# A transformer block on one core: moved DMA loads, a moved projection tile and a new order of carry, squares and SiLU

## The reference

```
x = x + layernorm(attn(layernorm(x)))      # no scale or shift in any layernorm
x = x + layernorm(ffn(layernorm(x)))

attn: q, k, v = split(x @ w_qkv.T + b_qkv) # 16 heads of 32
      per chunk of 128 tokens, state S (32 x 32 per head):
      inter = (q * decay_q) @ S
      intra = ((q @ k.T) * dmask) @ v
      S     = lam_c * S + (k * decay_k).T @ v
      out   = (inter + intra) @ w_out.T + b_out
ffn:  silu((x @ gate) * gs) * ((x @ up) * us) @ down * ds    # weights rounded to fp8 e4m3, inner width 1536
```

## Time and profile before

| | |
|---|---|
| median of 3 timed runs | 1053.86 us (1053.73 to 1054.44) |
| the profiled execution | 1055.15 us |
| its span, first to last instruction | 1053.4 us |
| PE busy with matmuls | 962.4 us, 91% |
| DVE, ACT, POOL busy | 684.1, 527.3, 687.5 us |
| mean granted TensorE clock | 0.98 of full speed |
| one slot in the steady state | 44.60 us |

### The profile page before, as it was taken

How to read it: one execution, slowest core, us unless ns; L and a number is a source line. 1 busy time by engine, 2 the same in 40 slices (tenths; PEclk the granted TensorE clock), 3 DMA queues, 4 the chain that set the end, 5 groups by cost and what they waited for, 6 DMA issues and landing times.

```text
span 1053.4 us, 21805 instructions
## 1 busy us (share of the span) xinstructions
PE 962.4 (91%) x8388; PEld 704.9 (67%) x8388; DVE 684.1 (65%) x1340; ACT 527.3 (50%) x997; POOL 687.5 (65%) x839
## 2 busy tenths in 40 slices
PE   1987989999777899999999999999999999999996
PEld 1755757777555577676776767767677686766764
DVE  6757766775475776576767657677766776756322
ACT  3534746675444554563545645456454464544421
POOL 2649887887555566685666857658576685856633
PEclk9988999999889899999999999999999999999999
DMA  9567889989999869387492864929559395621100
GB/s 341 134 206 202 247 210 227 245 209 216 244 226 229 162 136 191 76 156 128 107 189 76 165 118 114 184 75 170 112 123 166 87 169 112 130 61 41 38 24 21
DMA packets 297496, 159.79 MB, mean 152 GB/s; under 512 B 141616, under 2 KB 272688, under 8 KB 297264
## 3 DMA queue, kind: packets, MB, share of 16 engines
q1 hardware_dynamic: 296672, 157.86, 67.6%
q10 hardware_dynamic: 720, 0.54, 0.2%
HBM read 82.86 MB, written 41.94 MB: 118 GB/s over the span
## 4 chain that ended last, share of the span: by engine, by line
PE 58%; ACT 12%; DVE 9%; issue 8%; POOL 6%; SPq 5%; DMA 2%; POOLq 0%; DVEq 0%; ACTq 0%
PE bank L799 20%; PE bank L813 16%; PE att L776 8%; PE bank L707 4%; PE bank L692 4%; ACT w_pool L543 3%; PE att L692 3%; ACT y L441 2%; DVE w_pool L1329 2%; ACT hl L441 2%; ACT att_pool L497 2%; DVE stats L1198 2%; SPq L340 1%; DMA dram_qk<-qk_hl 1%; DVE state_hl L1269 1%
## 5 line engine op out<-in xcount | busy, mean ns | idle before, releaser
L799 PE MATMUL bank<-f_pool,gate_q 128*128 128x256 f16 x1536 | 184.2, 273 | 17.7 <-ACT w_pool L543 16.7
L799 PE MATMUL bank<-f_pool,up_q 128*128 128x256 f16 x1536 | 184.5, 274 | 0.0
L813 PE MATMUL bank<-down_q,w_pool 128*128 128x512 f16 x768 | 168.5, 379 | 11.0 <-DVE w_pool L1329 10.6
L799 PEld LDWEIGHTS bank<-f_pool,gate_q 128*128 128x128 f16 x1536 | 146.9, 98 | 41.8 <-ACT w_pool L543 21.0
L949 POOL TENSOR_TENSOR att_pool<-p,att_pool 128x512 f16<-128x512 f32 x128 | 145.7, 1161 | 39.1 <-ACT att_pool L497 39.1
L799 PEld LDWEIGHTS bank<-f_pool,up_q 128*128 128x128 f16 x1536 | 150.9, 98 | 18.0
L1329 DVE SCALAR_TENSOR_TENSOR w_pool<-bank,us_t,w_pool 128x256 f32<-128x256 f32 x192 | 84.1, 479 | 120.5 <-PE bank L799 70.6
L963 POOL TENSOR_TENSOR w_pool<-w_pool 128x512 f16<-128x512 f32 x96 | 111.8, 1164 | 65.8 <-ACT w_pool L549 65.8
L887 POOL TENSOR_TENSOR rstd<-mv,eps_t 128x1 f32<-128x1 f32 (+1 forms) x112 | 27.8, 248 | 176.8 <-DVE mv L1201 158.7
L813 PEld LDWEIGHTS bank<-down_q,w_pool 128*128 128x128 f16 x768 | 73.8, 98 | 99.9 <-DVE w_pool L1329 13.0
L497 ACT CAST att_pool<-p 128x512 f16<-128x512 f32 x128 | 75.6, 618 | 91.7 <-DVE p L1239 91.7
(11 more groups left out here) (139 smaller groups left out, 1823.1 us busy)
## 6 DMA issues: line engine op xcount, KB each, us to landing
xr<-in_x SPq DMA_DIRECT2D x32, 512.0 KB, 4.4
dram_qk<-qk_hl SPq DMA_DIRECT2D x64, 256.0 KB, 5.3
att_pool<-dram_qk SPq DMA_DIRECT2D x64, 256.0 KB, 6.8
f_pool<-dram_qk SPq DMA_DIRECT2D x64, 256.0 KB, 7.0
dram_v<-vv SPq DMA_DIRECT2D x32, 256.0 KB, 2.7
dram_kd<-kd_hl SPq DMA_DIRECT2D x32, 256.0 KB, 3.1
qn_pool<-dram_qk SPq DMA_DIRECT2D x32, 256.0 KB, 7.7
out_x<-w_pool SPq DMA_DIRECT2D x32, 256.0 KB, 2.1
```

The lines of the kernel that those rows point to most:

```text
L799: ins = nc.tensor.matmul(b[:, j * TOK:(j + 1) * TOK], w[:, k, o * P:(o + 1) * P], x1_hl[:, v % 2, part, k], start=(k == 0 and part == 0), ...
L813: ins = nc.tensor.matmul((b_gate, b_up)[t][:, :], h_hl[:, part, k, t * P:(t + 1) * P], down_q[:, k], start=(k == 0 and part == 0), stop=(k ...
```

## The change

No instruction of arithmetic is added or removed. Moved are:

- on SP, the load of unit 0 from behind lead block 12 to behind lead block 8, and the load of unit 1 from early call 0 to behind lead block 13;
- on PE, the sums of squares of pieces 0 to 4 by one block (5 joins 6 in block 8), and DVE's first maximum from block 6 to 7;
- in the early calls, ACT's k_hi ahead of y_normalise and x1_hi, POOL's residuals and x1_lo back, DVE's x1_moments behind carry and state;
- in a slot, the second tile of the output projection (`project(u, 1)`) behind `gate_up(v, 2)`, carry and state of the second chunk behind `gate_up(v, 4)`, SiLU ahead of y_normalise and x1_hi, state_hi and state_lo back; `down` waits for the last SiLU in place of the last product.

```diff
--- before.py
+++ after.py
@@ -204,6 +204,12 @@
         def squares(n):
             buf = o32 if n % 2 else y32
             return buf[:, :].rearrange("p t d -> p (t d)").bitcast(F16)[:, 0:I]
+
+
+
+        SUMMED = {3: (0,), 4: (1,), 5: (2,), 6: (3,), 7: (4,), 8: (5, 6), 9: (7,), 10: (8,), 11: (9,), 12: (10,),
+                  13: (11,)}
+        NORMS = {7: 0, 10: 1}
 
 
         def x_src(n):
@@ -397,8 +403,10 @@
             turn_x(1)
             for k in range(LEAD):
                 ahead(k)
-                if k == LEAD - 2:
+                if k == LEAD - 6:
                     load_unit(0)
+                if k == LEAD - 1:
+                    load_unit(1)
 
             for s in range(units + 2):
                 n, u, v = s + LEAD, s - 1, s - 2
@@ -408,7 +416,7 @@
                     spill_kd(n - 1)
                 if v >= 1:
                     store(v - 1, 0)
-                if s + 1 < units:
+                if 2 <= s + 1 < units:
                     load_unit(s + 1)
                 if v >= 1:
                     store(v - 1, 1)
@@ -595,17 +603,17 @@
                 q_hi(n, 0)
                 probs_hi(s, 0, 1)
                 q_hi(n, 1)
+                k_hi(n, 2)
                 if u >= 0:
                     y_normalise(u, 0)
                     y_normalise(u, 1)
-                k_hi(n, 2)
                 probs_hi(s, 1, 0)
+                k_hi(n, 3)
+                probs_hi(s, 1, 1)
+                state_hi(s, 1)
                 if u >= 0:
                     x1_hi(u, 0)
                     x1_hi(u, 1)
-                k_hi(n, 3)
-                probs_hi(s, 1, 1)
-                state_hi(s, 1)
                 o_hi(s)
 
             def slot(s):
@@ -626,27 +634,27 @@
                     probs_hi(s, 0, 1)
                 silu(v, 1)
                 h_hi(v, 1)
+                silu(v, 2)
                 if projects:
                     y_normalise(u, 0)
-                silu(v, 2)
+                h_hi(v, 2)
                 if projects:
                     y_normalise(u, 1)
-                h_hi(v, 2)
+                silu(v, 3)
                 if attends:
                     probs_hi(s, 1, 0)
-                silu(v, 3)
                 if projects:
                     x1_hi(u, 0)
                 h_hi(v, 3)
                 if attends:
                     probs_hi(s, 1, 1)
+                silu(v, 4)
                 if projects:
                     x1_hi(u, 1)
-                silu(v, 4)
-                if attends:
-                    state_hi(s, 1)
                 h_hi(v, 4)
                 silu(v, 5)
+                if attends:
+                    state_hi(s, 1)
                 h_hi(v, 5)
                 if attends:
                     o_hi(s)
@@ -803,7 +811,7 @@
 
             def down(v, t):
                 if t == 0:
-                    pe.wait_ge(h_d, 6 * v + 6)
+                    pe.wait_ge(silu_d, 6 * v + 6)
                     pe.wait_ge(h_lo_d, 6 * v + 5)
                 for k in range(IT):
                     if t == 0 and k == IT - 2:
@@ -820,8 +828,8 @@
                 project_qk(k, 1)
                 project_qk(k, 2)
                 project_qk(k, 3)
-                if 2 <= k < 14:
-                    sum_squares(k - 2)
+                for n in SUMMED.get(k, ()):
+                    sum_squares(n)
                 project_v(k, 0)
                 project_v(k, 1)
 
@@ -857,16 +865,18 @@
                 gate_up(v, 1)
                 if projects:
                     project(u, 0)
+                gate_up(v, 2)
+                if projects:
                     project(u, 1)
-                gate_up(v, 2)
                 if attends:
                     attend(s, 0)
                     scores(s, 1, 0)
                 gate_up(v, 3)
                 if attends:
                     scores(s, 1, 1)
+                gate_up(v, 4)
+                if attends:
                     carry_and_state(s, 1)
-                gate_up(v, 4)
                 gate_up(v, 5)
                 if attends:
                     attend(s, 1)
@@ -1016,18 +1026,17 @@
                 if u >= 0:
                     for t in range(T):
                         inverse_std_of(LN_Y, u, t)
-                    for t in range(T):
-                        residual(u, t)
+                state_decay(s, 1)
                 probs_lo(s, 1, 0)
                 if u >= 0:
                     for t in range(T):
-                        inverse_std_of(LN_X1, u, t)
-                state_decay(s, 1)
-                if u >= 0:
-                    x1_lo(u, 0)
+                        residual(u, t)
                 probs_lo(s, 1, 1)
                 if u >= 0:
-                    x1_lo(u, 1)
+                    for t in range(T):
+                        inverse_std_of(LN_X1, u, t)
+                    for t in range(T):
+                        x1_lo(u, t)
 
             def slot(s):
                 n, u, v = s + LEAD, s - 1, s - 2
@@ -1357,10 +1366,8 @@
                     scale_wout()
                 if k == 5:
                     split_wout()
-                if k == 6:
-                    norms(0)
-                if k == 10:
-                    norms(1)
+                if k in NORMS:
+                    norms(NORMS[k])
                 k_lo(k, 2)
                 if k < 12:
                     rounded(k)
@@ -1389,16 +1396,17 @@
                 k_lo(n, 2)
                 out_sum(s, 0)
                 masked(s, 1, 0)
-                if u >= 0:
-                    for t in range(T):
-                        x1_moments(u, t)
                 k_lo(n, 3)
                 masked(s, 1, 1)
                 v_sum(n, 0)
                 carry_and_state(s, 1)
+                if u >= 0:
+                    x1_moments(u, 0)
+                v_sum(n, 1)
+                if u >= 0:
+                    x1_moments(u, 1)
+                state_lo(s, 1)
                 o_max(s, 0)
-                v_sum(n, 1)
-                state_lo(s, 1)
                 out_sum(s, 1)
                 o_max(s, 1)
                 scale_o(s)
@@ -1421,8 +1429,9 @@
                 product(v, 1)
                 if projects:
                     y_moments(u, 0)
+                product(v, 2)
+                if projects:
                     y_moments(u, 1)
-                product(v, 2)
                 if projects:
                     x1_moments(u, 0)
                 if attends:
@@ -1433,16 +1442,16 @@
                 product(v, 3)
                 if attends:
                     masked(s, 1, 1)
-                    carry_and_state(s, 1)
                     o_max(s, 0)
                 product(v, 4)
                 if attends:
-                    state_lo(s, 1)
+                    carry_and_state(s, 1)
                 product(v, 5)
                 if attends:
                     out_sum(s, 1)
                     o_max(s, 1)
                     scale_o(s)
+                    state_lo(s, 1)
                     o_lo(s)
                 y2_scale(v, 0)
                 y2_moments(v, 0)
```

More of the change, by code:

```diff
@@ L642, in slot @@
                     probs_hi(s, 1, 1)
+                silu(v, 4)
                 if projects:
                     x1_hi(u, 1)
-                silu(v, 4)
+                h_hi(v, 4)
+                silu(v, 5)
                 if attends:
                     state_hi(s, 1)
-                h_hi(v, 4)
-                silu(v, 5)
                 h_hi(v, 5)
```

## The result

The changed kernel takes **1089.5 us** (median of 4 runs, 1089.13 to 1090.43) against 1053.8 us: ratio 1.034, 95% interval 1.032 to 1.036. The span went from 1053.4 to 1087.7 us, +34.3. The direction and the range held (1062 to 1094); the middle, 1080, was 9.5 us low, and the result lies 1.5 us outside the range of the likeliest case alone.

The account below looks back on a forecast made before the run. TensorE bounds the slots, with GpSimd's list nearly dense up to `down`. Loads +14, early calls -17.6, slots +29.3, slot 16 +1.7 and slot 17 -1.1 sum to +26 on 1053.9: 1080 us, range 1062 to 1094.

Parts of the forecast that it names:

- likeliest case: Slots, loads and early calls as forecast: 1080 us, range 1070 to 1088 taken alone, chance 0.6.
- Slots (b): Second projection tile behind block 2 ends 3.50 us later, GpSimd's list follows, `down` starts later: +2.14 us a slot.
- Slots (a): `down` waits for the last SiLU, state_lo and carry moved: both TensorE slot waits go, at most 1.86 us a slot.
- Loads: Lead blocks: early load of unit 0 delays spills, TensorE waits 12 us at block 10's squares; +14, bounds 9 and 18.
- Squares (c): Lead blocks: squares summed a block later take 3 waits away (11.9 us), costed at nothing.
- Slot 16: Slot that only projects: same GpSimd chain without probabilities, about +1.7 us.
- Early calls and slot 2 (d): Early calls into slot 2: earlier loads and k_hi cut TensorE's idle time; -17.6 us, bounds -10 and -26.
- The port rule: VectorE with two SBUF inputs and GpSimd lock each other out; moving state_lo would give VectorE 2.15 us a slot.
- The hidden load: Rival: slots as forecast, but the load behind lead block 8 is hidden; 1066 us, chance 0.15.
- The faster case: Rival: GpSimd's chain doesn't hold `down`, only the wait at attend stays, -0.85 us a slot; 1035 us, chance 0.12.
- The extra 1 us a slot: Rival: VectorE, waiting for the residual, makes GpSimd wait, 1 us more a slot; 1094 us, chance 0.1.
- the clock drop in a slot: Rival: new waits of about 1 us lower the clock in the slots; little chance, no time of its own.

Follow-up runs that it names:

- the version without the losses: The change with projection joined, y_normalise as before, h_lo(4) ahead of x1_lo(1), unit 0 loaded in pieces behind spills: 1014.4 us, 0.962; also called the best version.
- the experiment: The change with the order of ScalarE, GpSimd and VectorE in the two early calls as before: 1092.3 us, 1.037.

## Why the prediction was right, and where it missed

**Slots (b), +2.14 a slot.** Right, by the mechanism named. Measured +29.7 against +29.3 over 13 slots; the period is 46.70 as forecast, with waits of 0.93 for y (0.85), 1.43 for p (1.4) and 0.96 for the low half (1.1), and none at block 5. The slots that end a sequence lost more than the others, as worked out: 2.70 us each (forecast 2.5), against 2.10 in the others (2.14). The experiment with h_lo ahead of x1_lo shows that POOL's list is what holds `down` in the change: it takes out 1.10 us a slot, and nothing else was touched.

**Slots (a), "by themselves remove both slot waits: at most 1.86 us a slot".** Wrong as a description of the edit, harmless in the sum. Mean slot from `down` of slot 2 to `down` of slot 15, over kernels whose slots differ in these two things (their lead blocks and early calls differ too, but lie ahead of this stretch):

| order of the rest | projection joined | projection split |
|---|---|---|
| as before | 44.21 | 47.70 |
| the change's | 44.63 | 46.50 |
| the change's, y_normalise as before | 43.08 | 46.52 |

The split costs 3.44 us in the bottom row, one block (3.50): there POOL's list comes last with and without it. It costs 1.87 in the middle row, where y_normalise had already delayed that list. The 3.49 of the old order go another way, over ACT and DVE, with POOL's list done 1.4 us ahead of `down`. The rest of the order is worth 1.1 us when y_normalise stays where it was, and costs 0.4 when it moves behind h_hi(2); with the split it gives 1.2 in either form. I had the sum right since I worked it from the end of the second tile down POOL's list, and with the split nothing in the new order delays that list. The part for (a) by itself was not 1.86 but a loss of 0.4. To gain the two waits of a full slot takes y_normalise in its old place (44.60 to 43.23) and h_lo(4) ahead of x1_lo(1) as well (42.71 in the version without the losses, 1.89 less).

**Loads.** Right: 15.9 against 14, one wait of 13.46 where I had 12, behind v_hi and dram_v as named. The spill went out at 215.52 (214.9), the squares ended at 229.81 + 1.48 = 231.3 (229.8), and these 1.5 us are the wait that I had too short. The slow V projection cost 1.5 us where I had 2.3, and the squares' own matmuls 0.6 (1.46 for 0.82) where I had nothing. That the load causes it is shown twice: alone it makes +15.5, and back in its place it gives back 8 us net, with the wait at the squares gone.

**Squares (c), nothing.** Right: 1089.5 with and without. With the load late again the lead blocks end at 271.88 - 1.50 = 270.38, 2.2 us ahead of the kernel before, so without the stall the squares may be worth something. As kernels with the same lead blocks end them up to 2.0 us apart, that is not shown.

**Slot 16, +1.7.** Near in size (+1.3), but not by the chain named; that is luck. `down` waits 0.18 us for POOL there. PE loses its time to blocks 4 and 5, whose SiLU stand behind y_normalise and x1_hi in ACT's list: 3.4 us of waits in all, where before it had 1.49 and 0.97.

**Early calls and slot 2 (d), -17.6.** The step that failed, in size: -11.3. To block 0 of slot 2 I laid out 64 us; it took 355.16 - 288.40 = 66.8. For slot 2 I had 4.8 less and 2.1 more; it is 38.01 against 37.13 us, 0.9 more. What I missed is one transfer with two that wait for it. I had the chain from the last state over x1_hi and x1_lo to the turn, but took block 0 as held by little; it was held 5.10 us, and the lower clock made the first 16 matmuls 1.7 us longer. And I didn't see that ACT's o_hi waits for that same turn, so that SiLU 0 and 1 were late as well: PE waits 0.92 us at block 1 and 0.52 us at block 2. These and the slow matmuls are 3.1 of the 3.6 us that I had too little in slot 2. Of the -11.3, the load of unit 0 alone is worth -6.9 (116.07 to 109.15). With the load of unit 1 early and the change's slot order besides, it is 107.10 (-2.1), and the new order of the early calls brings 104.77 (-2.3). So the early order pays, and my reading in the experiment that it makes the turn late was wrong.

**The port rule.** I named the Trainium skill (SBUF — State Buffer, "SBUF: two separate sides") for state_lo and held it against the rows of POOL. The move does take state_lo from 3.31 to 1.15 us, as the rule has it. In the change that bought no time at `down`, since POOL came last. In the kernel with the split alone DVE is what `down` waits for; whether the move would pay there, no run tests.

**Rivals.** The hidden load is excluded by the 13.46 us wait. The faster case needed the second tile's end to h_lo 4 in under 16.1 us; it did not happen in the change. With h_lo 4 ahead of x1_lo it got 1.10 us shorter, which still left the slot 1.0 us above the 44.60 of before. The price of that rival was off too: it kept only the wait at `attend`, and the one at `scores` (1.44 us) stays as well. The extra 1 us a slot didn't come, nor did the clock drop in a slot (1.00).

**Open.** The load of unit 1 was not moved alone. Up to block 0 of slot 2, ahead of any slot order, the kernel with both loads early and the old early order takes 358.36 - 289.92 = 68.4 us, the one with unit 0's alone 358.91 - 288.07 = 70.8; the 2.4 us between them are the nearest figure. What the squares' remaining 6 us of waits in the best version hang on was not tried.

## What to carry to other kernels

- Find the engine whose list is dense up to the point where PE waits, and count from the event that starts it. Moving that event later by one block cost one block here (3.44 of 3.50 us) where the list came last before and after, while the list's engine was busy 67% of the slot. Where something else had delayed the list already, it cost 1.87.
- Price each line of a reordering on its own. One move in ACT's order (the two y_normalise one place later each, the second behind h_hi) turned a gain of 15 us into a loss of 6, and it was harmless in the company of another edit.
- A row of the profile that joins two DMA issues can hold a wait between them. Look at each issue before a queue is blamed.
- A burst of DMA issues belongs where its queue waits anyway. The twelve of one load in one piece made the lead blocks 15.9 us longer; in five pieces they make them 3.1 longer (276.50 - 0.88 = 275.6 against 272.55).

## What the runs showed of the hardware

- The transposing DMA of k holds SP's queue for 6.97 us behind eleven other DMAs of the load, and for 2.29 us when it is issued without them (best version, at 262.99).
- After 5.10 us of idle PE took 3.58 us for 16 matmuls in place of 1.92; the granted clock there was 0.50. After waits of 0.9 to 1.2 us, three in each slot, nothing of the kind shows (1.00 over the slot).
- Four state_lo on DVE take 1.15 us with POOL idle and 3.35 us beside it.
